# A map stage whose second norm needs no mean: an extra channel row through the scratch maps, variances in four column groups, Z2 with a patch's channels in a run

## What is computed

```python
x = x + conv(_ln_c(x), ...)      # x: (2, 96, 256, 256), norm over the 96 channels
t = t + ffn(_ln_t(t), ...)       # per token: 96 -> 384 -> 96, 8-bit float products

# conv(x):
#  16 x 16 windows at step 14 (19 x 19 per image), layernorm, 4-head attention in each window,
#  + residual, windows averaged back onto the map     -> x2
#  y = gelu(layernorm(x2) @ fc1 + b)                  96 -> 192
#  y = y + gelu(depthwise 5x5(y) + b)
#  out = y @ fc2 + b + x2
```

## Time and profile before

| what | value |
|---|---|
| median of 3 runs | 10127.56 us (10114.91 to 10147.24) |
| profiled execution | 10134.36 us, its span 10132.5 us |
| mean granted TensorE clock | 0.945 |
| busy share of the span | PE 87%, PE weight load 53%, DVE 55%, ACT 45%, POOL 19% |
| DMA | 609.18 MB, queue q1 24.5% of 16 engines |

### The profile page before, as it was taken

One profiled execution on the slowest core, in us unless ns is written; L12 is line 12 of the kernel. 1 busy time (PEld: TensorE's weight loads), 2 busy tenths in 40 slices (PEclk: granted clock), 3 DMA queues, 4 the chain that ended last, 5 costly groups with the idle time before them and its releaser, 6 DMA issues.

```text
span 10132.5 us, 200877 instructions
## 1 busy us (share of the span) xinstructions
PE 8854.8 (87%) x73708; PEld 5392.1 (53%) x73708; DVE 5580.2 (55%) x10186; ACT 4596.0 (45%) x8600; POOL 1891.9 (19%) x1660
## 2 busy tenths in 40 slices
PE   7776999999999999996898989898989898989898
PEld 3333444444444444443566666666666666666665
DVE  5655777777777777774434343434443444443444
ACT  2222555555555555553344444444444444444443
POOL 0000333333333333332010101010101010101010
PEclk8887999999999999997999999999999999999999
DMA  4433333333333333335111111111111111111110
GB/s 113 121 114 95 86 86 86 89 85 88 94 79 94 86 86 86 89 94 58 29 30 36 30 36 30 36 30 36 30 36 30 36 30 36 30 36 30 36 30 21
DMA packets 473959, 609.18 MB, mean 60 GB/s; under 512 B 169864, under 2 KB 409066, under 8 KB 448650
## 3 DMA queue, kind: packets, MB, share of 16 engines
q1 hardware_dynamic: 473496, 602.66, 24.5%
HBM read 394.17 MB, written 165.49 MB: 55 GB/s over the span
## 4 chain that ended last, share of the span: by engine, by line
PE 34%; DVE 8%; ACT 6%; issue 4%; SPq 1%; DVEq 0%; ACTq 0%; DMA 0%; POOLq 0%; POOL 0%
PE P L1248 6%; PE P L1239 5%; PE P L1115 5%; PE P L1165 4%; ACT H L1313 4%; PE P L1090 3%; PE P L1095 3%; DVE H L1471 2%; PE P L1128 2%; PE P L1123 2%; DVE H L1464 2%; DVE Z L1486 2%; PE P L1268 1%; ACT L1301 1%; ACT L1323 1%
## 5 line engine op out<-in xcount | busy, mean ns | idle before, releaser
L796 DVE TENSOR_REDUCE NM<-P 128x2 f32<-128x512 f32 x2888 | 1910.5, 688 | 743.6 <-PE P L633 734.6
L748 ACT ACTIVATE PROB<-P 128x512 f32<-128x512 f32 x2888 | 1491.3, 603 | 1213.7 <-PE P L648 1213.7
L1165 PE MATMUL P<-FC,XN 97*126 97x192 f32 x5408 | 1121.3, 356 | 140.3 <-ACT Y L1323 139.4
L1064 POOL TENSOR_TENSOR T<-T,Y 96x512 f16 (+1 forms) x260 | 299.0, 1150 | 4679.4 <-DVE Y L1475 4679.4
L1165 PEld LDWEIGHTS P<-FC,XN 97*126 97x126 f32 x5408 | 1019.2, 209 | 265.8 <-ACT Y L1323 176.4
L633 PE MATMUL P<-KB,QB 32*128 32x256 bf16 x5776 | 868.1, 281 | 195.5 <-DVE QF L790 106.9
L648 PE MATMUL P<-QF,KS 32*128 32x256 f32 x11552 | 958.0, 414 | 0.0
L1435 DVE TENSOR_TENSOR X<-X,P 96x512 f32<-96x512 f32 x364 | 248.8, 683 | 1188.4 <-PE P L1090 1188.4
L1307 ACT ACTIVATE SQ<-Z 96x512 f32<-96x512 f32 x260 | 163.7, 630 | 1497.2 <-DVE Z L1451 1282.8
L633 PEld LDWEIGHTS P<-KB,QB 32*128 32x128 bf16 x5776 | 249.4, 94 | 1075.5 <-DVE QF L790 528.0
L656 PE MATMUL P<-PROB,V 128*32 128x256 f32 x11552 | 803.1, 397 | 1.5 <-ACT PROB L748 1.5
(11 more groups left out here) (133 smaller groups left out, 13387.8 us busy)
## 6 DMA issues: line engine op xcount, KB each, us to landing
RBC<-sums SPq DMA_DIRECT2D x456, 160.0 KB, 3.1
X<-x2map SPq DMA_DIRECT2D x52, 1344.0 KB, 8.4
XHS<-xhat SPq DMA_DIRECT2D x76, 768.0 KB, 8.4
RNS<-rnorm SPq DMA_DIRECT2D x38, 1536.0 KB, 9.4
x2map<-XHS SPq DMA_DIRECT2D x76, 768.0 KB, 5.2
T<-in_x SPq DMA_DIRECT2D x52, 960.0 KB, 11.1
out<-T SPq DMA_DIRECT2D x52, 960.0 KB, 4.9
X<-in_x SPq DMA_DIRECT2D x32, 1536.0 KB, 13.2
```

The source lines that it names most:

```text
L748: A.activation(PROB[:, par, u, :], P[:, B_ST[u], :], ACT.Exp, scale=DQ ** -0.5).then_inc(act_exp, 1)
L796: V_.tensor_reduce(NM[:, :, 32 * u + DQ], P[:, B_S[u], :].rearrange("p (a m) -> p a m", a=2), axis=AX.X, op=ALU.max).then_inc(dve_max, 1)
L1165: m = M.matmul(P[0:KW, 5 + (r + 2) % 3, i * MLP:(i + 1) * MLP], xnf[:, RI * WX * w:RI * WX * w + KW], FC1[:, :], start=True, stop=True)
```

## The change

The attention stage carries one more channel. `WP` gets a 97th column, the mean of its 96 columns, which are then made free of their mean; so the 97th output row of `project` is the mean over the channels and the other 96 are centred. `XH`, `xhat` and `x2map` get a 97th row; `xhat`'s is filled with zeros at the start. `store` and `fetch` keep their text (`XH[:, ...]`, `xhat[:, ...]`), so they now move 97 rows. The map stage reads 96 centred rows as `X2`; the mean row of the strip is loaded into `TM[C]` by a DMA of its own, copied by POOL into row C of `Z` (`means`), and added by `fc2` through a row of ones in `FC2`. `mean2` and `centre2` are gone. Variances are collected in four column groups of 32 with 128 columns each; a copy to SBUF (`sum2`, `sum3`) and a product with `REP` (`gather2`, `gather3`) bring them together. The standard deviations and their reciprocals have 128 columns (`CV`) and not 256. In `Z2` [128, NWIN, C] the channels of one patch lie in a run. Squares, windows and `std` are at other places of the ACT and PE queues.

```diff
 # attention stage
-        XH = sb("XHS", [C, 2, PATCH, W])
+        XH = sb("XHS", [C + 1, 2, PATCH, W])
-        WP = sb("WP", [128, C])
+        WP = sb("WP", [128, C + 1])
...
+            sp.dma_start(xhat[C, :, :].rearrange("b n -> (b n)").rearrange("(p e) -> p e", p=128),
+                         ACCO[:, 0:B * H * W // 128 // PATCH, :].rearrange("c x r -> c (x r)")).then_inc(z_stored, 16)
+            sp.wait_ge(z_stored, 16)
...
-            zrow = ACCO[0:C, 0:B * 2 * W // PATCH, :].rearrange("c x r -> c (x r)").rearrange("c (b n) -> c b n", b=B)
+            zrow = ACCO[0:C + 1, 0:B * 2 * W // PATCH, :].rearrange("c x r -> c (x r)").rearrange("c (b n) -> c b n", b=B)
...
-                T.matmul(P[0:C, B_CK, :], WP[:, :], af[:, ck(c)], start=True, stop=True).then_inc(pe_out, 1)
+                T.matmul(P[0:C + 1, B_CK, :], WP[:, :], af[:, ck(c)], start=True, stop=True).then_inc(pe_out, 1)
...
-                V_.tensor_tensor(x, P[0:C, B_CK, :].rearrange("c (w r) -> c r w", r=PATCH), x, ALU.add).then_inc(dve_out, 1)
+                V_.tensor_tensor(x, P[0:C + 1, B_CK, :].rearrange("c (w r) -> c r w", r=PATCH), x, ALU.add).then_inc(dve_out, 1)
 # map stage
-        Z2 = sb("Z2", [128, C, NWIN])
-        Z = sb("Z", [C, 2, WX * NWIN * RO])
+        Z2 = sb("Z2", [128, NWIN, C])
+        Z = sb("Z", [C + 1, 2, WX * NWIN * RO])
...
+                sp.dma_start(TM[C:C + 1, bass.ds(half_of(sp, u + 2), TO)],
+                             x2map[C:C + 1, bass.ds(bx, 1), bass.ds(own, TO)].rearrange("c a n -> c (a n)")).then_inc(xo_loaded, 16)
...
+            def means(u):
+
+                G.tensor_copy(Z[C:C + 1, 0, 0:TO].rearrange("c (x y) -> c x y", y=RO),
+                              TM[C:C + 1, bass.ds(half_of(pool, u), TO)].rearrange("c (y x) -> c x y", x=W)).then_inc(pool_m, 1)
...
-            def mean2(v, j):
...
-                for c in (2 * j, 2 * j + 1):
-                    m = M.matmul(P[0:C, 7, 0:CW], SSEL[:, NCH - 1 - c:NCH - 1 - c + C], SQ[:, 2 + j % 2, (c % 2) * CW:(c % 2 + 1) * CW],
-                                 start=(c == 0), stop=(c == RI - 1))
+                for q in range(4):
+                    c = 4 * j + q
+                    m = M.matmul(P[32 * q:32 * q + 32, 4, 0:CV], SSEL[:, NV - 1 - c:NV - 1 - c + 32], SQ[:, 2 + j % 2, q * CV:(q + 1) * CV],
+                                 start=(j == 0), stop=(j == NL - 1))
...
+            def gather2(v):
+                pe.wait_ge(dve_vs, v + 1)
+                M.matmul(P[0:C, 5, 0:CV], REP[:, :], VS[0][:, :], start=True, stop=True).then_inc(pe_rep, 1)
...
+                for q in range(4):
+                    m = M.matmul(P[0:C, 5 + j % 2, q * CV:(q + 1) * CV], BSEL[:, 4 * j + q, :], RB[0][:, :], start=True, stop=True)
...
-                    m = M.matmul(P[0:C, j % 2, 0:px.stop - px.start], FC2[:, half, :], Z[:, half, px], start=(half == 0), stop=(half == 1))
+                    m = M.matmul(P[0:C, j % 2, 0:px.stop - px.start], FC2[0:C + 1 - half, half, :], Z[0:C + 1 - half, half, px], start=(half == 0), stop=(half == 1))
...
 # first_half, PE: var2 beside fc1 and the first convolution group, gather2 after that group
+                    if k % 2 == 1:
+                        beside(var2, k // 2)
...
-                    if q < 4:
-                        beside(mean2, *range(2 * q, min(2 * q + 2, NL)))
...
-                    if 1 <= q < 5:
-                        beside(var2, *range(2 * q - 2, min(2 * q, NL)))
...
 # second_half, PE: windows between the parts of mean3 and var3
-                beside(windows, 0, 1, 2)
+                beside(windows, 0, 1)
+                mean3(half3, n5, nx, 2)
                 var3(n5, 0)
-                mean3(half3, n5, nx, 2)
+                beside(windows, 2)
+                mean3(half3, n5, nx, 3)
                 var3(n5, 1)
...
+                beside(windows, 5)
+                gather3(n1)
+                beside(windows, 6)
                 pe.wait_ge(dve_parts3, n1)
...
 # ACT, first_half and second_half
+                    if v is not None and k % 2 == 0:
+                        square2(v, k // 2)
...
-                    A.activation(Z2[:, 2 * GP * q:2 * GP * (q + 1), :].rearrange("p (a c) w -> p a (c w)", a=2),
-                                 P[:, b:b + 2, 0:GP * NWIN], ACT.Gelu).then_inc(act_conv, 1)
+                    A.activation(Z2[:, :, 2 * GP * q:2 * GP * (q + 1)].rearrange("p w (a c) -> p w a c", a=2),
+                                 P[:, b:b + 2, 0:GP * NWIN].rearrange("p a (c w) -> p w a c", w=NWIN), ACT.Gelu).then_inc(act_conv, 1)
+                    if v is not None and q == 0:
+                        std2(v)
...
 # DVE, first_half
-                for j in range(NL):
-                    centre2(v, j)
+                sum2(v)
                 dve.wait_ge(act_std, v + 1)
-                parts(STD, RB[0], CW, steps2, dve_parts2, lambda i: back(n7, i - 1))
-                back(n7, 5, 6)
+                parts(STD, RB[0], CV, steps2, dve_parts2)
+                back(n7, *range(NB))
...
 # kernel()
-    xhat = nc.dram_tensor("xhat", (C, B, H * W), fp32, kind="Internal").ap()
+    xhat = nc.dram_tensor("xhat", (C + 1, B, H * W), fp32, kind="Internal").ap()
-    x2map = nc.dram_tensor("x2map", (C, B, HP * W), fp32, kind="Internal").ap()
+    x2map = nc.dram_tensor("x2map", (C + 1, B, HP * W), fp32, kind="Internal").ap()
```

More of the change, by code:

```diff
@@ L1029, in _ @@
                 hold(sp, sp_passed, dve_xn, sp.snap(u * NL + 2 * NL))
+                hold(sp, sp_passed, pool_x, sp.snap(u + 2))
                 fetch_map(u + 2)
@@ L1134, in spread3 @@
                     pe.wait_ge(dve_t8, n5 + j)
-                for c in (2 * j, 2 * j + 1):
-                    m = M.matmul(P[0:C, 4, (c % 2) * CW:(c % 2 + 1) * CW], BSEL[:, c, :], RB[1][:, :], start=True, stop=True)
+                for q in range(4):
+                    m = M.matmul(P[0:C, 4, q * CV:(q + 1) * CV], BSEL[:, 4 * j + q, :], RB[1][:, :], start=True, stop=True)
                 m.then_inc(pe_bc3, 1)
@@ L1245, in first_half @@
                     for i in range(2 * GP):
+                        if q == 0 and i == GP:
+                            beside(var2, NL - 1)
                         c = 2 * GP * q + i
@@ L1345, in beside @@
                         windows(v, *rs)
-                for j in range(NF):
+                square3(n5, 0)
+                square3(n5, 1)
+                for j in range(2, NF):
+                    beside(j - 2)
                     square3(n5, j)
-                act.wait_ge(pe_var3, n5 + NF)
-                A.activation(STD3[:, :], P[0:C, 4, 0:CW], ACT.Sqrt, bias=EPS[:, 0:1]).then_inc(act_std3, 1)
-                beside(0, 1, 2, 3, 4, 5, 6, 7, 8)
+                beside(3)
+                act.wait_ge(pe_rep3, n1)
+                A.activation(STD3[:, :], P[0:C, 4, CV:2 * CV], ACT.Sqrt, bias=EPS[:, 0:1]).then_inc(act_std3, 1)
+                beside(4, 5, 6, 7, 8)
                 hidden16(n5, 0)
@@ L1409, in _, with parts @@
             V.memset(Y1[96:128, :, :], 1.0).then_inc(dve_w, 1)
-            def parts(std, rb, n, v0, done, fill):
+            def parts(std, rb, n, v0, done):
                 steps = [0]
@@ L1526, in second_half @@
                 out16(n5, NF - 1)
-            for j in range(NL):
-                centre2(0, j)
+            sum2(0)
             dve.wait_ge(act_std, 1)
-            parts(STD, RB[0], CW, 1, dve_parts2, lambda i: None)
+            parts(STD, RB[0], CV, 1, dve_parts2)
             for j in range(NL):
@@ L1579, in constants @@
     inside = np.stack([inside[t:t + RI].T.reshape(-1) for t in tops])
-    return ident, stat, bcast, share, qrows, taps, inside
+    pick = np.zeros((C, NV - 1 + 32), f)
+    pick[:, NV - 1] = 1.0 / C
+    rep = np.zeros((128, C), f)
+    spread = np.zeros((C, NV, C), f)
+    for c in range(NV):
+        for k in range(3):
+            spread[32 * k + c, c, :] = 1.0
+            for g in range(4):
+                rep[32 * g + c, 32 * k + c] = 1.0
+    return ident, stat, bcast, share, qrows, pick, rep, spread, taps, inside
 def kernel(**inputs):
@@ L1588 @@
     arrays = {f"in_{n}": np.ascontiguousarray(a) for n, a in inputs.items()}
-    for n, a in zip(("ident", "stat", "bcast", "share", "qrows", "taps", "inside"), constants()):
+    for n, a in zip(("ident", "stat", "bcast", "share", "qrows", "pick", "rep", "spread", "taps", "inside"), constants()):
         arrays[f"const_{n}"] = a
```

178 lines of the change are left out of this document (96 added, 82 removed).

## The result

The kernel after takes **14103.69 us** (median of 4 runs, 14097.9 to 14112.83) against 10137.4 us before (10114.91 to 10151.69, 4 runs): ratio 1.392, 95% interval 1.3886 to 1.3946. It is slower, as forecast. The forecast was 16600 us with a range of 14000 to 18200; the time lies inside, 104 us above its lower end.

The account below looks back on a forecast made before the run. It took PE, busy about nine tenths of the time, as the bound, with DMA seemingly idle. 10134 + 7280 (attention) - 810 (map) = 16604 us, given as 16600 us; own range 15400 to 17700, stated range 14000 to 18200.

Parts of the forecast that it names:

- One DMA engine for 97 rows: Attention stage: engines must divide the rows, 97 is prime, so each half strip gets one engine; attention +7280 us.
- The 25-row weights: Depthwise weights' load: DMA share 0.48 against 1.89 for 96 rows, read as the row count limiting the engines.
- 52.5 us a half strip: Attention `store` on one engine, priced at 15.1 GB/s, its pace among 16; a fetch was put at 49.9 us.
- the fast bound: Attention half strip on one engine at the trace's fastest rate: 34.5 us, attention +4200 us.
- the third rival: Attention: one engine alone is quicker than one of 16; 34.5 us a half strip, 218 us a strip, 13900 us; chance 0.06.
- The bound row of 23 GB/s: Fastest rate in the earlier trace, 369 GB/s with longer runs, 23 GB/s an engine: 34.5 us a half strip.
- the two faster rivals: Attention: small copies pass, 14250 us, chance 0.10; one engine alone is quicker, 13900 us, chance 0.06.
- Who waits: Attention: DVE stops in `keys16` and `shares` behind three half strips, then one; 284.9 us a strip against 97.3.
- The second rival: Attention: small copies pass the big ones, the loaded engine sets the pace; 227 us a strip, 14250 us; chance 0.10.
- Cold PE, 3 us a strip, and the start: Attention: slow PE restarts after stops add 110 us; first fetches, zero fills and zero row add about 140 us.
- The map stage, -15.8 us a strip: Map stage: seven terms for means, variances, transposes, spreading and second half; -810 us over 51 strips, -500 to -1000.
- Spreading: Map stage, first half: spreading in 48 pieces and not 24 costs +1.2 us a strip.

Follow-up runs that it names:

- split: The kernel after, with half strips and zero fills each moved as two transfers, 96 rows and one row: 9310.08 us, ratio 0.919.
- rows98: The kernel after, with an unread 98th row in both maps and `XH`, half strips again one transfer: 9283.11 us.
- rows106: The kernel after, with 106 rows in both maps and `XH`, all moved, for 2 engines: 11588.35 us.
- rows116: The kernel after, with 116 rows in both maps and `XH`, all moved, for 4 engines: 10364.15 us.
- rows102: The kernel after, with 102 rows in both maps and `XH`, all moved, for 6 engines: 9764.18 us.
- z2old: rows98 with `Z2` back to [128, C, NWIN], so transposes read weights in strides of 208 bytes: 9328.49 us.
- fetch96: The kernel after, with fetches of 96 rows and stores still of 97, the mean row's fetch left out: 11610.87 us.
- order2: rows98 with PE and ACT taking the map stage's second half in the order of the kernel before: 9474.96 us.

## Why the prediction was right, and what was mis-sized

1. **One DMA engine for 97 rows.** Right, and it is what decides the outcome. The 25-row weights, at a share of 0.48 against 1.89, were enough to read it from; a stop at share 0.07, split and rows98 show it.
2. **52.5 us a half strip.** The mis-sized term, and the reason for 14104 and not 16600. It measured 37.0 us, 21.5 GB/s on the one engine, close to the fast bound of 34.5 us and to the third rival, which I gave 0.06. I had taken the pace of one engine among sixteen (15.1 and 15.9 GB/s) for the pace of one alone. rows106, rows116 and rows102 show that each keeps 21.5 GB/s with two and four at work and falls to 17.5 in a store with six. What then holds them back, no run here shows. The bound row of 23 GB/s was the nearer one, and its price in the prediction is wrong by its own sum: 34.5 us give 218 us a strip, as in the third rival, and so 38 x 120.8 = +4590 us for the strips alone, not +4200.

   The forecast's own range (half strips of 43 to 58 us, 15400 to 17700) missed. The time lies in the stated range only because that was stretched to 14000 for the two faster rivals, by a margin of 104 us, and that is luck.
3. **Who waits.** Right in place: `keys16` and `shares`, three half strips in a row, then one. The sum of the strip with 37.0 in the place of 52.5 and 49.9 is 4 x 37.0 + 80.1 = 228 us; 224.1 was measured, as the work between the stops took 38.9 and 37.0 us and not 40.6 and 39.5. The mechanism had a part that the prediction lacked, the queue that stands at the issue. Whether the small copies would also wait on the loaded engine cannot be told apart here, for they are not issued before it is nearly free. The second rival (small copies pass) gives 14250 us and so almost the measured time, but is wrong: it has no stops, and DVE stands for 64.4 and 34.5 us at steps 10 and 11 and for 26.1 us at step 1.
4. **Cold PE, 3 us a strip, and the start.** The stage runs at a mean clock of 0.70 (0.96 before), yet the work between the stops is no longer than before (39.4 and 37.2 us in the mean of all strips, 39.7 and 40.2 before), so the 110 us were not there to be added. The "16 window products" from which they were taken are sixteen records of eight products, which changes nothing in the ratio. The stage starts 130 us later (forecast 140). The stores of side 1 close the sum: the first comes at 1270.94 and not 1089.51 us, so 181 us later in all; 36 strips follow at 224.4 and not 98.7 us, 4525 us; the rest takes 58 us more. That is the measured 4764 us. The single strip of the earlier trace rows (97.3 us) was one of the shorter ones, and made 38 strips look 42 us dearer; two fetches left out at the end are worth 74 us at 37 us each, and not 100.
5. **The map stage, -15.8 us a strip.** Right: the stage lost 810 us, and from the start of the first fc1 to the end of the last the loop went from 5178 to 4356 us, 16.1 us a strip over 51. The chain that ended last in one strip answers to the earlier trace rows:

```profile
12013.35 1.95 PE P L1152 x4
...
12017.46 0.36 PE P L1158 x8
...
12030.64 1.46 ACT H L1351
...
12051.23 1.53 PE P L1278 x4
...
12063.25 1.07 PE P L1291 x32
...
12066.68 1.28 ACT L1339
...
12068.36 1.28 ACT L1376
...
12077.43 1.06 PE P L1307 x8
...
12085.70 3.13 PE P L1144 x8
```

Term by term. fc1 with the variances beside it takes 12063.25 - 12051.23 = 12.0 us, +2.4 (forecast +1.9: four products took 0.36 and not 0.27 us). The convolution takes 14.2 us where it and what lay in it took 25.9: -11.7 (forecast -12.9 + 1.0 for the gather and the table loads, which stand between 12066.68 and 12069.64). The transposes take 8.3 where they took 12.3: -4.0 (forecast -2.0, bound -5). From the first `mean3` (12013.35) to the first `hidden16` (12030.64) are 17.3 us, where the trace of before has 22.6 (7064.94 to 7087.50): -5.3 (forecast -3.0 - 2.0). Spreading takes 0.45 us, no more than before (forecast +1.2). These sum to -18.6 us in a strip of 83.5 us, and that is one of the 6 shortest of 51; most take 85.2.

Over all strips of both traces (the means of 49 or 50) the terms are +2.4 for fc1, -11.8 for the convolution, -3.8 for the transposes, only -3.5 from `mean3` to `hidden16`, and +0.5 for the rest, in all -16.2 us. So the sum is close to -15.8 in part by errors that cancel: the transposes and the spreading gave 3.0 us more than forecast, and the second half, fc1 and the rest 2.6 us less. (Also, 3.5 x 1.73 us for `var2` is 6.1 and not 6.2.)

6. **What hid in the rows of before.** Part of the 181 ns a transpose and of the 5.48 us of windows was not their own price but the halved clock. Two windows of the kernel before, in its transposes and in its window products, and below them a whole map strip of after and the same place (behind `parts`) in its next strip:

```profile
7049.00:7051.00 2.00, 2.00 (x11) 1.95 (x11) 1.77 (x5) 0.00 (x0) 0.00 (x0) 0.50 0.00 0
...
7079.00:7081.00 2.00, 1.83 (x6) 1.83 (x7) 1.81 (x8) 1.12 (x4) 0.00 (x0) 0.50 0.00 0
```

```profile
12002.00:12085.00 83.00, 75.04 (x776) 50.90 (x776) 36.73 (x79) 45.56 (x72) 15.89 (x7) 1.00 0.16 41
...
12112.00:12118.00 6.00, 6.00 (x22) 5.24 (x22) 1.62 (x3) 2.88 (x4) 0.00 (x0) 0.50 0.00 0
```

The kernel before fell to the lower level (1.2 GHz) twice in this strip, each time after PE had stood (1.97 and 2.44 us in its timeline). In the strip shown after stays at 2.4 GHz through all 83 us, but that is not its rule: in 44 of 50 strips its clock is low for over half a microsecond between `mean3` and `hidden16`, too. In the mean a strip of before has 7.3 us at the lower level and one of after 3.5 us. Of this, 1.9 us of before lay in the transposes, in 27 of 49 strips, and in after none does; the 27 take 12.1 to 12.5 us for that stretch and the 22 others 11.7, so in the mean the clock explains 0.3 of the 3.8 us won there, and the new layout 0.5 (z2old). The rest fits the forecast's reason, that the deviation and the reciprocal are done earlier, but no run takes that apart.

## What to carry to other kernels

Before you add a row to a tile that is moved by DMA, factor the new row count: from 96 to 97 rows cost 4794 us here, while the same row as a transfer of its own, or one more row of padding, cost next to nothing. A DMA share that is low says nothing of this, since one engine at work is a share of 0.07 here; look at how long a transfer, and the instruction issued behind it, take. And price one engine by the fastest pace per engine in the trace, not by its part of sixteen.

## What the runs showed of the hardware

- On 512-byte runs a transfer on one DMA engine moved 22 GB/s (share 0.07), on two 43 (0.14), on four 86 (0.29), on six 105 in a store (0.39) and 127 in a fetch (0.43), and on sixteen 242 and 255 (0.91 and 0.95).
- With one engine loaded, SP does not go on issuing: the fetch behind the store took 34.5 us to issue, also in fetch96, where it has 96 rows. With two engines it took 17.9 us, with four 9.3, with six 6.3, with sixteen 0.7.
- PE idle for 2.68 us (up to 12027.95) in after left the granted clock at 1.00; 2.67 us at the same place of the next strip (up to 12111.45) were followed by 0.50, and 2.34 us in order2 too. The length of the idle alone does not decide it.
